# Tiles of 15 rows per partition in place of 16, three products per PSUM bank, in a message-passing kernel on one core

## The reference: what is computed

```python
h = relu(layernorm(x))
mats = (attr @ W_bond + b_bond).reshape(E, 32, 32)      # one matrix per edge
for _ in range(4):                                      # four steps
    msg = einsum('eij,ej->ei', mats, h[dst])            # gather by dst
    agg = segment_sum(msg, src, N)                      # sum by src
    h = gru_cell(agg, h)
x = x + h
g = relu(layernorm(x))
deg = segment_sum(1, dst, N)
norm = rsqrt(deg)[src] * weight * rsqrt(deg)[dst]
out = x + segment_sum(g[src] * norm[:, None], dst, N)
```

## Time and profile before

| | |
|---|---|
| median of three runs | 30029.33 us (30025.87 to 30030.98) |
| the profiled execution | 30022.3 us, its span 30020.5 us |
| PE, DVE, ACT, POOL busy | 49%, 36%, 26%, 67% of the span |
| mean granted TensorE clock | 0.644 of full speed |

### The profile page before, as it was taken

How to read it: one execution, slowest core, us unless ns; L and a number is a source line. 1 busy time by engine, 2 the same in 40 slices (tenths; PEclk the granted TensorE clock), 3 DMA queues, 4 the chain that set the end, 5 groups by cost and what they waited for, 6 DMA issues and landing times. The chain is left out here.

```text
span 30020.5 us, 295457 instructions
## 1 busy us (share of the span) xinstructions
PE 14803.7 (49%) x72221; PEld 11376.6 (38%) x72222; DVE 10783.8 (36%) x35992; ACT 7681.6 (26%) x24111; POOL 20078.1 (67%) x21002
## 2 busy tenths in 40 slices
PE   3389999744554444444454544445454400000089
PEld 3366666533333333333333333333333300000089
DVE  8789999722222222222222222222222300000044
ACT  9977777611111111111111111111111100000000
POOL 0077777677777677777677777677777677777700
PEclk6655555577777677777677777677777655555555
DMA  3000000111111111111111111111111111111111
GB/s 146 0 14 16 16 16 16 20 28 28 29 28 28 27 28 28 29 28 29 27 28 28 29 28 29 27 28 29 28 28 29 25 46 43 43 43 42 36 36 40
DMA packets 1766515, 932.08 MB, mean 31 GB/s; under 512 B 1175189, under 2 KB 1669316, under 8 KB 1757636
## 3 DMA queue, kind: packets, MB, share of 16 engines
q0 software_dynamic: 671776, 322.48, 7.6%
q1 hardware_dynamic: 523940, 533.80, 6.3%
q10 hardware_dynamic: 570240, 70.85, 1.5%
HBM read 650.58 MB, written 280.42 MB: 31 GB/s over the span
## 5 line engine op out<-in xcount | busy, mean ns | idle before, releaser
L954 POOL DMA_INDIRECT h_rows<-h_table,rec x13824 | 13042.9, 943 | 4331.3 <-issue 4096.8
L1102 PE MATMUL outer<-a_masked,h_by_quarter 128*128 128x136 f32 x27648 | 5123.0, 359 | 8937.9 <-DVE h_by_quarter L995 8937.9
L1102 PEld LDWEIGHTS outer<-a_masked,h_by_quarter 128*128 128x128 f32 x27648 | 4850.1, 260 | 9413.9 <-issue 9413.9
L1148 ACT COPY outer_sums<-outer 128x272 f32<-128x272 f32 x6912 | 2642.0, 385 | 14585.7 <-PE outer L1102 13880.1
L995 DVE TENSOR_TENSOR h_by_quarter<-h_rows,gates 128x2048 f32<-128x2048 f32 x864 | 1976.8, 2288 | 7206.5 <-DMA h_rows<-h_table,rec 7206.5
L1367 POOL DMA_INDIRECT messages_by_bucket<-ms,ix x3456 | 3457.9, 1001 | 1073.5 <-issue 1052.2
L731 POOL DMA_INDIRECT edges_by_node<-row,place x3125 | 2993.6, 958 | 1237.8 <-issue 1237.8
L1078 PE MATMUL msg_psum<-outer_sums,w_bond_blocks 128*128 128x512 f32 x7344 | 3665.6, 647 | 0.0
L988 DVE TENSOR_TENSOR a_masked<-rec,gates 128x2176 f32<-128x2176 f32 x864 | 2090.2, 2420 | 4368.9 <-PE outer L1102 4347.0
L550 PE MATMUL plook<-next_free,ot_f 128*128 128x98 f32 x6250 | 2228.3, 460 | 0.0
L1078 PEld LDWEIGHTS msg_psum<-outer_sums,w_bond_blocks 128*128 128x128 f32 x7344 | 1564.0, 225 | 1562.0 <-issue 1561.7
(11 more groups left out here) (247 smaller groups left out, 20451.0 us busy)
## 6 DMA issues: line engine op xcount, KB each, us to landing
h_rows<-h_table,rec POOLq DMA_INDIRECT x13824, 2.4
rec<-edges_by_node SPq DMA_DIRECT2D x1080, 168.0 KB, 2.3
carry_flags<-carry_flags SPq DMA_DIRECT2D x270, 256.0 KB
chunk_sums<-scan_t ACTq DMA_DIRECT2D x864, 64.0 KB
g_of_rows<-g_of_every_chunk SPq DMA_DIRECT2D x216, 256.0 KB, 3.3
messages_by_bucket<-ms,ix POOLq DMA_INDIRECT x3456, 2.2
mr<-messages_by_bucket SPq DMA_DIRECT2D x202, 264.0 KB, 2.7
messages_by_bucket<-zeros SPq DMA_DIRECT2D x33, 1600.0 KB, 40.4
```

What stands on the lines that cost most here:

```text
L954: pool.indirect_dma_start(out=hb[j][:, u, :], out_offset=None, in_=ht, in_offset=bass.IndirectOffsetOnAxis(ap=rec[j][:, u, W_DST:W_DST + 1 ...
L1102: last = pe.matmul(pt[g % RING][:, at:at + KC], hq[j % 2][:, u, :, :].rearrange("p q d -> p (q d)"), am[j % 2][:, u, :, :].rearrange("p k ...
L1148: act.copy(ts[b][:, :, at:at + w].rearrange("p k (u c) -> p u k c", c=CPT), pt[g % RING][:, 0:GPB * KC].rearrange("p (u k c) -> p u k c", ...
```

## The change

One iteration handles 15 tiles, and three tiles share a PSUM bank, so an iteration has NB = 5 bank fills. T3 is rounded up to a multiple of GI * J3 = 60, which gives 3420 tiles, 228 iterations and 57 groups; the number of groups of a step is odd now, and the last group stands alone behind the loop over pairs. A group has 480 columns in place of 512, and the tiles that hold them transposed use 120 partitions. Since 15 is no power of two, the row and the iteration of a slot are worked out by a multiplication with 4370 and a shift by 16 in place of masks and shifts; `place_r3_b` has five instructions in place of three. POOL's second wait stands ahead of gather 9 (HALF) and asks for three bank fills of the iteration before. `weigh` still stands ahead of bank fill NB // 2, which is 2 now.

```diff
-J3 = P // CPT
+J3 = 15
+DIV15 = 4370
...
-    T3 = up(-(-(E + N * (CH - 1)) // P), 2 * GI * J3)
+    T3 = up(-(-(E + N * (CH - 1)) // P), GI * J3)
...
+    USES = ((NGR + 1) // 2, NGR // 2)
...
-                        ch(dve.tensor_scalar(ti[:], si[:], LS, J3 - 1, ALU.logical_shift_right, ALU.bitwise_and))
+                        ch(dve.tensor_scalar(ti[:], si[:], LS, None, ALU.logical_shift_right))
                         ch(dve.tensor_copy(slot[:], ti[:]))
-                        ch(dve.scalar_tensor_tensor(out=quarter[:], in0=quarter[:], scalar=float(QP * J3), in1=slot[:],
+                        ch(dve.tensor_scalar(ti[:], slot[:], float(DIV15), None, ALU.mult))
+                        ch(dve.tensor_scalar(ti[:], ti[:], 16, None, ALU.logical_shift_right))
+                        ch(dve.tensor_copy(tile_at[:], ti[:]))
...
-            GPB = 2
+            GPB = 3
             NB = J3 // GPB
             RING = 4
+            HALF = (NB + 1) // 2 * GPB
...
+                    body(s * IT3 + (NGR - 1) * GI, s * NGR + NGR - 1, 0, NGR // 2, NGR - 1, 2)
...
                                 for u in range(J3):
-                                    if u % (J3 // 2) == 0 and not (past == 0 and j < 2):
-                                        pool.wait_ge(s_t, n0 * NB + (j * NB + NB + (NB // 2 if u else 0)))
+                                    if u in (0, HALF) and not (past == 0 and j < 2):
+                                        pool.wait_ge(s_t, n0 * NB + (j * NB + NB + u // GPB))
                                         hold(pool)
...
                                     for u in range(g * GPB, (g + 1) * GPB):
                                         at = (u - g * GPB) * KC
-                                        last = pe.matmul(pt[g % RING][:, at:at + KC], hq[j % 2][:, u, :, :].rearrange("p q d -> p (q d)"),
+                                        last = pe.matmul(pt[(j * NB + g) % RING][:, at:at + KC], hq[j % 2][:, u, :, :].rearrange("p q d -> p (q d)"),
                                                          am[j % 2][:, u, :, :].rearrange("p k c -> p (k c)"), start=True, stop=True)
...
-                            act.copy(sct[b][:], px[:]).then_inc(s_sc, 1)
+                            act.copy(sct[b][0:NT], px[0:NT]).then_inc(s_sc, 1)
...
-                            sp.dma_start(gl[b][:, j, :].rearrange("c (q d) -> c q d", d=D),
+                            sp.dma_start(gl[b][0:NT, j, :].rearrange("c (q d) -> c q d", d=D),
```

More of the change, by code:

```diff
@@ L110, in gnn_program @@
     GW = GI * NT
-    assert T3 * P < BIG and T2 * P < BIG and HB <= P and HB * D <= 7 * 512 and NT == P and T2 % 4 == 0
+    USES = ((NGR + 1) // 2, NGR // 2)
+    assert T3 * P < BIG and T2 * P < BIG and HB <= P and HB * D <= 7 * 512 and NGR % 2 == 1 and T2 % 4 == 0
+    assert T3 * DIV15 < 1 << 24 and all(t * DIV15 >> 16 == t // J3 for t in range(T3))
     r3 = nc.dram_tensor("edges_by_node", [T3 * P, W3], F32).ap()
@@ L605, in _ @@
                 def _(dve):
-                    KP = 18
+                    KP = 20
                     AHEAD = 3
@@ L1005, in scan, with group @@
                                                    sc[1 - b][:, GW - 1:GW], ALU.mult, ALU.add).then_inc(s_scan, 1)
-                        def group(n0, ng, b, i, g, past):
+                        def group(n0, ng, b, i, g, past, last=False):
                             if past == 2:
-                                scan(ng - 2, b, s * (NGR // 2) + i - 1)
+                                scan(ng - 2, b, s * USES[b] + i - 1)
                             for j in range(GI):
@@ L1013, in group @@
                                 spread_h(n0 + j, ng, j)
-                            if b == 0:
+                            if b == 0 and not last:
                                 make_a(n0 + GI, ng + 1, 0, 0)
@@ L1022, in step @@
                             group(s * IT3 + i * (2 * GI) + GI, s * NGR + i * 2 + 1, 1, i, i * 2 + 1, 2)
-                        scan(s * NGR + NGR - 2, 0, s * (NGR // 2) + NGR // 2 - 1)
-                        scan(s * NGR + NGR - 1, 1, s * (NGR // 2) + NGR // 2 - 1)
+                        make_a(s * IT3 + (NGR - 1) * GI, s * NGR + NGR - 1, 0, 0)
+                        group(s * IT3 + (NGR - 1) * GI, s * NGR + NGR - 1, 0, NGR // 2, NGR - 1, 2, last=True)
+                        scan(s * NGR + NGR - 2, 1, s * USES[1] + USES[1] - 1)
+                        scan(s * NGR + NGR - 1, 0, s * USES[0] + USES[0] - 1)
                         dve.wait_ge(s_tr, s * NGR + NGR + 2)
@@ L1105, in step @@
                         groups_of_step(pe, s, group)
-                        turn_scan(s * NGR + NGR - 2, 0)
+                        turn_scan(s * NGR + NGR - 2, 1)
                         for part in range(GI):
-                            weigh(s * NGR + NGR - 1, 1, s * (IT3 * NB) + IT3 * NB + RING, part)
-                        turn_scan(s * NGR + NGR - 1, 1)
+                            weigh(s * NGR + NGR - 1, 0, s * (IT3 * NB) + IT3 * NB + RING, part)
+                        turn_scan(s * NGR + NGR - 1, 0)
                         for g in range(NG):
@@ L1213, in message_groups @@
                     spread(0, 0, 0)
-                    with eng.Fori(0, NGR // 2 - 1) as i:
+                    with eng.Fori(0, NGR // 2) as i:
                         spread(i * 2 + 1, 1, i)
@@ L1218, in message_groups @@
                         rows(i * 2 + 1, 1, i)
-                    spread(NGR - 1, 1, NGR // 2 - 1)
-                    rows(NGR - 2, 0, NGR // 2 - 1)
-                    rows(NGR - 1, 1, NGR // 2 - 1)
+                    rows(NGR - 1, 0, NGR // 2)
                 @block.sync
@@ L1320, in spread @@
                         act.wait_ge(s_gst[b], i * (16 * GI))
-                        act.copy(gc[b][:], pgb[:]).then_inc(s_gc, 1)
+                        act.copy(gc[b][0:NT], pgb[0:NT]).then_inc(s_gc, 1)
                         act.wait_ge(s_gc, g + 2)
@@ L1342, in spread @@
                         for j in range(GI):
-                            last = pe.transpose(pgt[:, j * NT:(j + 1) * NT], gl[b][:, j, :], ident_f[:])
+                            last = pe.transpose(pgt[:, j * NT:(j + 1) * NT], gl[b][0:NT, j, :], ident_f[0:NT, 0:NT])
                         last.then_inc(s_gt, 1)
@@ L1348, in spread @@
                         for j in range(GI):
-                            last = pe.transpose(pgb[:, j, :], gpm[:, j, :], ident_f[:])
+                            last = pe.transpose(pgb[0:NT, j, :], gpm[:, j, :], ident_f[:])
                         last.then_inc(s_gtb, 1)
```

37 lines of the change are left out of this document (20 added, 17 removed).

## The result

The changed kernel takes 31420.36 us, the median of six runs (31414.04 to 31423.37); the kernel before took 30029.92 us beside it (six runs, 30025.87 to 30030.98). The ratio is 1.0463, 95% interval 1.0449 to 1.0476: slower. The forecast was 31410.

The account below looks back on a forecast made before the run. POOL's gathers were taken to bound the steps. Profiled 30022.3 + 1376 (steps) - 47 (last message stage) + 57 (placing) = 31408, with 7 us to the median 31415, said as 31410; range 30800 to 31600.

Parts of the forecast that it names:

- What bounds it: Steps: POOL issues gathers without a stall, 1.248 us each; its wait in mid-iteration has a margin of 1.54 us.
- How early a wait must be answered: POOL's wait in the steps: POOL needs 0.79 us more than another engine to start after the answer.
- The order on PE: Steps: PE has 8 records of `weigh` ahead of the third bank fill that POOL's wait ahead of gather 9 needs.
- x: Steps: time from PE's first product to the third bank fill's first one, 6.14 to 7.71 us, 7.4 needed for balance.
- The hold: Steps: iterations settle at the spacing of the clock's rises, 20.48 us, a stall of 1.75 us each.
- Rival 1: Steps: the clock's rise keeps wandering, so the stall is its mean, 1.24 us per iteration; 30960 us, chance 0.27.
- Rivals 2 to 4: Steps: no stall (29853 us, chance 0.1), stall of 0.8 us (30567, 0.08), weighing all at 1.2 GHz (33070, 0.03).
- rival 2: Steps: POOL's sequencer reads ahead and swallows a late answer, so no stall; 29853 us, chance 0.1.
- Part 1: Fewer tiles: 36 fewer gathers per step save 180 us in four steps, 36 fewer last-stage scatters save 47 us.
- The step's tail: End of each step: 1.5 us shorter, from a sixteenth less of 34 `weigh` records and smaller spreads.
- Part 3: Placing: two more DVE instructions cost 0.46 us in each of 124 iterations, +57 us, bounds 0 and 71.

Follow-up runs that it names:

- e4: Changed kernel with `weigh` and transposes behind the third bank fill, and placing's 21 DVE instructions one by one behind columns: 29719.11 us, 0.9887 of the kernel before.
- e10: Changed kernel with 12 more PE matmuls, results unread, behind each iteration's last bank fill: 29925.89 us, 0.9956 of the kernel before.
- e9: Changed kernel with one more DVE memset of 128x256 ahead of the spreading in every iteration: 31424.93 us, 1.0464 of the kernel before.
- e11: Changed kernel with POOL's wait ahead of gather 10 in place of 9, asking for the same three bank fills: 30016.02 us, 0.9983 of the kernel before.

## Why the prediction was right, step by step

- **What bounds it.** POOL's row of gathers at 1.248 us, and the margin of its wait in the middle of an iteration. Right: the gathers between the waits are still 1.248 apart, and the time is in the gap ahead of gather 9, 2.99 us from start to start in place of 1.248.
- **How early a wait must be answered, 0.79 us.** Measured 0.75, from ACT's copy to the gather. From the third bank fill's first product to that copy pass 0.89 us in both iterations shown, against 0.91 in the working.
- **The order on PE, and x.** x was to lie between 6.14 and 7.71 for eight records, 7.4 in the balance. The medians by j are 7.26, 7.54, 8.10 and 8.32, of which the last two have the transposes or the fifth matmul. The `e4` run shows that the order makes the stall, and `e10` that without the low clock it doesn't.
- **The hold.** 20.48 us an iteration and 1.75 of stall against 20.47 (20.480 where nothing slips) and 1.74. `e9` tells it from a sum that came out by accident: 0.20 us more in the chain changed nothing.
- **Rival 1, the mean of a wandering rise (20.0 us, 30960).** It falls: the rise doesn't wander. The Trainium skill, "TensorE: Matmul & The Clock Gate" ("What's actually happening"), puts the penalty of the ramp at under 1% of a typical kernel's span. The runs of this kernel disagree: with the low clock taken away it is at 0.9956 of the kernel before, with it at 1.0463. The section speaks of a number of slow matmuls that varies from run to run. In the kernel before it is the rise that varies, from iteration to iteration of one execution; in the changed one, whose bounding engine waits for PE, it doesn't.
- **Rivals 2 to 4.** No stall (29853), a stall of 0.8 us (30567) and no rise at all (33070) fall by the same rows; `e10`, with the low clock taken away, is what rival 2 describes: 29926 on a chip 27 us slower.
- **Part 1.** All other gathers still start 1.248 us apart, so the 144 fewer save their 180 us. The scatters gave -42.1 for -47: 3419 spacings of 1.3065 us in place of 1.3051 eat 5 us.
- **The step's tail, -1.5 us.** Wrong: it is near 0. From the last gather of a step to the first gather of sums pass 37.21 to 37.23 us; before it was 37.24 in the first step and 37.38 to 37.42 in the others, so the four tails shrank by 0.5 us together. The 34 records of `weigh` at the end did shrink, from 14.84 to 13.95 us, but in the first step they also start 0.7 us later behind the last gather (15.93 in place of 15.22). What the working left out stands ahead of them, the last iteration's own part of `weigh`. PE at the end of the first step, before and after:

```profile
10239.56 4.46 PE L1078 MATMUL msg_psum<-outer_sums,w_bond_blocks 128*128 128x512 f32 x10
10243.85 2.02 PE L1102 MATMUL outer<-a_masked,h_by_quarter 128*128 128x136 f32 x16
```
```profile
10646.42 5.58 PE L1090 MATMUL msg_psum<-outer_sums,w_bond_blocks 128*128 128x480 f32 x10
10651.84 2.25 PE L1114 MATMUL outer<-a_masked,h_by_quarter 128*128 128x136 f32 x18
```

  Ten records take 5.42 us where they took 4.29, since the hold puts the rise late in this iteration too. That the forecast of +1376 was met to within 1 us is luck, as two errors cancel. From first to last gather the four steps grew by 1375.6, 6.0 less than the 1381.6 of the working, most of it in the second step, where the hold slips; and the tails gave -0.5 in place of -6; the 1.3 us that are left over lie behind the tails.
- **Part 3, +57.** Measured +61.8, or 0.50 us in place of 0.46 for two instructions in each iteration. PE's wait for `bucket_place` grew from 262.8 us in 383 cases to:

```profile
PE nextb L535 <- DVE bucket_place L701: 318.6, 447, 1.7
```

  One of the two added instructions is dearer than the 0.17 to 0.19 us of rows 9, the product that is written as an integer:

```profile
4018.05 0.28 DVE L655 TENSOR_SCALAR slot_t<-slot 128x25 int32<-128x25 f32 x1
```

Open: what a wait one gather earlier costs on a chip like the first (it ran on the two others alone), and what makes these gaps. The edit of the order was not timed by itself on a chip without them; its part in `e4` is read from the steps.

## What to carry to other kernels

Where two engines are tied by a count of finished pieces, write the place of the wait and the order of the pieces by the same constant: here the wait asks for `HALF // GPB` fills and the order on PE followed `NB // 2`, equal for 8 fills and one apart for 5, and the one fill put 8 or 10 records of `weigh`, the first of them at the low clock, into the bounding engine's path. Before a wait gets tighter, work out the margin in both levels of the clock, and if the end of the awaited piece depends on a rise, ask where the loop's length settles rather than take the mean. The loop that was held like this did not answer to a small delay in the chain. By the same working a small saving there would not shorten it either, which no run shows. What did shorten it was to move the wait or the order out of reach of the clock.

## What the runs showed of the hardware

- A delay of 0.20 us in each of 912 iterations that looks serial cost nothing (31424.93 against 31420.36 us), since the granted clock's rise came 0.4 us sooner behind the first product, which took 0.20 us off the matmuls behind it, and the iteration stayed at 20.48 us.
- Superfluous matmuls made the kernel faster by 5%: PE busy for 1873 of 2000 us, granted clock 1.00, 29926 in place of 31420 us.
- From ACT's copy, which shows a bank fill done, to the gather that POOL's wait lets go pass 0.75 us in both iterations shown. In `e11`, where some waits stall and some don't, the shortest time by which a fill was done ahead of its gather's turn without a stall over 0.1 us is 0.65 us.
- Two chips ran the kernel before in some 36.7 ms in place of 30.03. On the first a scatter of placing is as long as elsewhere (0.96 us), but between one batch of 25 and the next POOL stands still, in the row shown for 30.58 us.
